# Six pairs' mean and variance computed by ScalarE instead of VectorE, and the one-hot rows of two chunks placed elsewhere

## The reference

```python
h = _layernorm(x, axis=-1) * (1 + ca) + sa
x = x + ga * _L0_attn_ref(h, w_qkv, w_out, b_out)
h = _layernorm(x, axis=-1) * (1 + cb) + sb
gate_probs = softmax(h @ Wg + bg)            # 8 experts, the best two are kept
x = x + gb * sum over the two experts of weight * (gelu(h @ W1 + b1) @ W2 + b2)
```

## Time and profile before

| | |
|---|---|
| median of 3 runs | 812.49 us (812.14 to 812.84) |
| the profiled execution's own time | 813.09 us |
| its span in the profile | 811.3 us |
| PE busy | 755.2 us, 93% of the span |
| DVE busy | 607.8 us, 75% |
| ACT busy | 463.8 us, 57% |
| POOL busy | 339.2 us, 42% |

### The profile page before, as it was taken

How to read it: one execution, slowest core, us unless ns; L and a number is a source line. 1 busy time by engine, 2 the same in 40 slices (tenths; PEclk the granted TensorE clock), 3 DMA queues, 4 the chain that set the end, 5 groups by cost and what they waited for, 6 DMA issues and landing times.

```text
span 811.3 us, 16803 instructions
## 1 busy us (share of the span) xinstructions
PE 755.2 (93%) x5848; PEld 689.0 (85%) x5848; DVE 607.8 (75%) x1325; ACT 463.8 (57%) x841; POOL 339.2 (42%) x291
## 2 busy tenths in 40 slices
PE   4889999999999899984699999999999999999992
PEld 4767778788888679972699999999999999999992
DVE  6899999988899735799576767676676876776652
ACT  4465555756645442359557566665565766765461
POOL 2441414323322101500255565656565555656553
PEclk9999999999999999977699999999999999999997
DMA  7500000000000124590353532626335244333332
GB/s 285 164 1 1 1 1 2 1 2 1 1 2 1 53 102 159 174 234 4 93 147 64 144 64 44 164 43 168 60 91 114 47 120 90 46 48 60 60 48 39
DMA packets 45650, 59.71 MB, mean 74 GB/s; under 512 B 8018, under 2 KB 38804, under 8 KB 45460
## 3 DMA queue, kind: packets, MB, share of 16 engines
q0 software_dynamic: 14400, 21.98, 15.1%
q1 hardware_dynamic: 31188, 36.93, 14.4%
HBM read 40.63 MB, written 18.27 MB: 73 GB/s over the span
## 4 chain that ended last, share of the span: by engine, by line
PE 74%; DVE 16%; issue 5%; ACT 2%; POOL 1%; DMA 1%; SPq 0%; DVEq 0%; POOLq 0%; ACTq 0%
PE ps L1681 24%; PE ps L1695 23%; PE ps L1492 7%; PE ps L1450 6%; PE ps L1513 3%; PE ps L1655 2%; DVE q_max L940 2%; PE ps L1578 2%; PE ps L1501 2%; DVE q_sum L947 2%; DVE k_blk L1050 2%; DVE q_exp L941 1%; ACT at_lo L788 1%; DVE ln_s L904 1%; PE ps L1560 1%
## 5 line engine op out<-in xcount | busy, mean ns | idle before, releaser
L853 ACT ACTIVATE hid<-ps,b_col 128x256 f32<-128x256 f32 (+1 forms) x232 | 105.9, 508 | 114.1 <-PE ps L1681 88.4
L1695 PE MATMUL ps<-w_hi,hid_hi 128*128 128x256 f32 x544 | 153.5, 282 | 0.0
L1695 PE MATMUL ps<-w_lo,hid_hi 128*128 128x256 f32 x544 | 151.2, 278 | 0.0
L1695 PE MATMUL ps<-w_hi,hid_lo 128*128 128x256 f32 x544 | 151.2, 278 | 0.0
L1371 DVE TENSOR_TENSOR hid_lo<-hid,hid_hi 128x512 fp32r<-128x512 f32 (+1 forms) x116 | 90.9, 784 | 76.1 <-ACT hid_hi L857 73.2
L1681 PE MATMUL ps<-xT_hi,w_hi 128*128 128x256 f32 (+1 forms) x464 | 140.9, 304 | 1.6 <-DVE xT_lo L1325 1.6
L1681 PE MATMUL ps<-xT_hi,w_lo 128*128 128x256 f32 (+1 forms) x464 | 140.7, 303 | 0.0
L1681 PE MATMUL ps<-xT_lo,w_hi 128*128 128x256 f32 (+1 forms) x464 | 140.6, 303 | 0.0
L539 POOL TENSOR_TENSOR q_n<-q_exp,q_rec 128x1024 f32<-128x1024 f32 x32 | 60.9, 1904 | 174.7 <-DVE q_rec L948 174.7
L614 POOL DMA_INDIRECT out<-y,y_id x68 | 117.0, 1721 | 40.1 <-POOL y_id L609 16.6
L602 POOL DMA_INDIRECT listed<-xrows,gid x87 | 95.5, 1097 | 42.3 <-POOL gid L598 24.6
(11 more groups left out here) (215 smaller groups left out, 1458.7 us busy)
## 6 DMA issues: line engine op xcount, KB each, us to landing
w_raw<-in_L_ffn_W SPq DMA_DIRECT2D x16, 1024.0 KB
x_all<-in_L_attn_x SPq DMA_DIRECT2D x8, 512.0 KB, 9.3
out<-x_all SPq DMA_DIRECT2D x8, 512.0 KB, 3.0
xrows<-x_all SPq DMA_DIRECT2D x8, 512.0 KB, 4.7
listed<-xrows,gid POOLq DMA_INDIRECT x87
out<-y,y_id POOLq DMA_INDIRECT x68
wqk_raw<-in_L_attn_w_qkv SPq DMA_DIRECT2D x2, 512.0 KB, 6.3
wqk_raw<-in_L_attn_w_qkv SPq DMA_DIRECT2D x1, 1024.0 KB, 10.5
```

Of the source, the lines that this page charges most:

```text
L853: ins = act.activation(hid[:, m, 0:T], src, ACT.Gelu_apprx_tanh, bias=b1_col[:, e, m:m + 1])
L1695: last = pe.matmul(ps[:, bank, 0:D], a, w_, start=m == 0 and st, stop=m == M - 1 and sp_)
```

## The change

DVE no longer takes statistics of pairs 8 to 13. ACT does it in a new function `moments(q)`, after `copy_T(q)`: for each of the two tiles an `Identity` with a constant scale, whose accumulator output is minus a sixteenth of the mean, and, after a wait for both, for each tile a `Square` whose bias is that number and whose accumulator output is the variance. DVE's `root(1)` waits for ACT's twelve variances and has one more instruction. ACT's `lo_hot(0)` moves from behind `copy_T(14)` to behind `copy_T(15)`, `soft(1)` now stands between `lo_hot(0)` and `lo_hot(1)`, and ACT's half of `lo_hot(7)` goes to DVE.

```diff
+ACT_PAIRS = range(8, 14)
...
+            def moments(q):
+
+                n = q - ACT_PAIRS[0]
+                after(act, s_mean, 2 * n)
+                after(act, s_var, 2 * n)
+                for i in range(2):
+                    t = 2 * q + i
+                    act.activation(bn_j[:, i, :], x_all[:, t, :], ACT.Identity, scale=-1.0 / (16 * D), accum_out=bn_m[:, t:t + 1]).then_inc(s_mean, 1)
+                act.wait_ge(s_mean, 2 * n + 2)
+                for i in range(2):
+                    t = 2 * q + i
+                    act.activation(bn_j[:, i, :], x_all[:, t, :], ACT.Square, scale=1.0 / 16, bias=bn_m[:, t:t + 1],
+                                   accum_out=bn_a[:, t, 1:2]).then_inc(s_var, 1)
...
-            def lo_hot(c, ks=range(2)):
+            def lo_hot(c):
...
+                if q in ACT_PAIRS:
+                    moments(q)
                 if q == 9:
                     soft(0)
-                if q == 14:
-                    lo_hot(0)
-            lo_hot(1)
+            lo_hot(0)
             soft(1)
-            lo_hot(2)
-            lo_hot(3)
-            for c in range(GCH, CHUNKS - 1):
+            for c in range(1, CHUNKS - 1):
                 lo_hot(c)
-            lo_hot(CHUNKS - 1, range(1))
...
-                dve.wait_ge(s_stat, q + 1)
+                dve.wait_ge(s_stat, q + 1 if q < ACT_PAIRS[0] else q + 1 - len(ACT_PAIRS))
...
-                if q % (GT // 2):
+                if q % (GT // 2) and q - 1 not in ACT_PAIRS:
                     dve.wait_ge(s_x1, 2 * q)
                     stats(q - 1)
-                    if q % (GT // 2) > 1:
-                        gathered(q - 2)
+                if q % (GT // 2) > 1 and q - 2 not in ACT_PAIRS:
+                    gathered(q - 2)
...
+                if g == 1:
+                    dve.wait_ge(s_var, 2 * len(ACT_PAIRS))
                 link(dve.tensor_scalar(bn_v[:, r], bn_a[:, r, 1], EPS, None, ALU.add))
                 inverse_root(meta[:, r, E], bn_v[:, r], bn_i[:, r], bn_t[:, r])
+                if g == 1:
+                    r = slice(2 * ACT_PAIRS[0], 2 * (ACT_PAIRS[-1] + 1))
+                    dve.scalar_tensor_tensor(meta[:, r, E + 1], bn_m[:, r], 16.0, meta[:, r, E], ALU.mult, ALU.mult)
+                    r = slice(r.stop, TILES)
...
-            lo_hot(CHUNKS - 1, 1)
-            hi_hot(CHUNKS - 1, (1, 0))
+            for k in (1, 0):
+                lo_hot(CHUNKS - 1, k)
+                hi_hot(CHUNKS - 1, (k,))
...
-                    if final and k == 1:
-                        pe.wait_ge(s_loD, 1)
+                    if final:
+                        pe.wait_ge(s_loD, n + 1)
```

More of the change, by code:

```diff
@@ L190, in adaln_block @@
         bn_a = sb("bn_a", [P, TILES, 2], F32, bb_stack)
+        bn_m = sb("bn_m", [P, TILES], F32, bb_stack)
+        bn_j = sb("bn_j", [P, 2, D], F32, bb_stack)
         bn_v = sb("bn_v", [P, TILES], F32, bb_stack)
@@ L248, in adaln_block @@
         s_stat = sem("s_stat")
+        s_mean = sem("s_mean")
+        s_var = sem("s_var")
         s_cT = sem("s_cT")
@@ L785, in lo_hot @@
                 after(act, s_idx, c - GCH + 1)
-                for k in ks:
+                for k in range(2):
                     for i in range(CH):
                         act.activation(at_lo[:, cc, k, i, :], iota_lo[:, :], ACT.Abs, scale=-1.0, bias=spot_lo[:, g, k, cc * CH + i:cc * CH + i + 1]).then_inc(s_abs, 1)
-                act.wait_ge(s_abs, (c * 2 + len(ks)) * CH)
-                one = at_lo[:, cc, 0:len(ks), :, :].rearrange("p k i c -> p (k i c)")
+                act.wait_ge(s_abs, (c * 2 + 2) * CH)
+                one = at_lo[:, cc, :, :, :].rearrange("p k i c -> p (k i c)")
                 act.activation(one, one, ACT.Relu, scale=-1.0, bias=1.0).then_inc(s_loA, 1)
```

## The result

The changed kernel takes 814.92 us (median of 7 runs, 813.29 to 817.41) against 812.55 us of the kernel before (7 runs beside them); ratio 1.0037, 95% interval 1.0026 to 1.0048. It is slower by 0.3 to 0.5%; 815.3 us was forecast. Its profiled execution was the longest of the seven, 817.41 us with a span of 815.7, so 4.3 us above that of before; a second one of the same kernel (816.49 us) is used beside it.

The account below looks back on a forecast made before the run. The prediction took `logits(15)` to gate `scale(1)` and ACT's queue behind the last copy, then sixteen matmuls, to set `ids`. Moving `ids` from 384.32 to 387.1 us (+2.8) gave 815.3 us, range 812.9 to 816.9.

Parts of the forecast that it names:

- What bounds: Before the `ids` write: `scale(1)` waits for `logits(15)`, so DVE's 4.0 us less work becomes idle time.
- The cost of the moments: ACT's added statistics in pairs 8 to 13: 2.29 us a pair, making `copy_T(14)` 0.54 us late.
- the ends 1.53 and 2.67: ACT's microseconds per pair for the statistics: accumulator output free, or a 0.284 us instruction each without overlap.
- The rows: ACT behind the last copy: chunks 0 to 6 without long waits, from 359.26 us to the last Relu's end at 384.06.
- The rival with the high clock: Clock stays high in the ping-pong and under the last matmuls: `ids` +0.5 us, 813.0 us, no difference; chance 0.15.
- DVE's saving: Rival, DVE's work ahead of `ids`: its 4.0 us come through in full, -4 us, 808.5 us; practically excluded.
- PE behind it: PE after ACT's last Relu: sixteen matmuls instead of four, 3.0 us taken (2.1 to 3.9), `ids` at 387.1 us.
- The other arm: PE's ranks and DVE: `place(1)` 0.1 to 0.7 us late, DVE ready at 385.0 to 385.6 us, hidden before `ids`.
- The rest follows rigidly: Everything behind `ids` was to move with its +2.8 us.
- The sum: Whole kernel: `ids` from 384.32 to 387.1 us, +2.8 us, giving 815.3 us against the median.
- No table was loaded for `Square`: Rival on ACT in the pairs: table loads for `Square`, about +16 us, 828; chance 0.10 together with a dear accumulator.
- sooner clock: Rival at the experts' first matmuls: the clock rises sooner, at most 2.8 us won, 812.5 us; chance 0.10.

Follow-up runs that it names:

- both experiments with the transposes ahead: PE transposes pairs 14 and 15 one pair ahead: ratio to the kernel before 1.0004 when added to the changed kernel, 0.9990 when added to the kernel before.
- rows-only kernel: Kernel before with only ACT's low one-hot rows and soft(1) moved and chunk 7's low rows all on DVE, statistics staying on DVE: ratio 1.0036.
- moments only: Kernel before with only the mean and variance of the six pairs moved to ACT, all one-hot rows in their old places: ratio 1.0013.
- before with transposes ahead: Kernel before with only PE's order changed, transposing pairs 14 and 15 one pair ahead: ratio 0.9990, interval 0.9976 to 1.0004.
- the combination: Changed kernel plus transposes of pairs 14 and 15 one pair ahead, ranks(1) before index(1), four of chunk 6's low rows on DVE: 809.33 us, ratio 0.9972.
- the combination without moments: The combination with DVE taking all statistics instead of ACT taking those of six pairs: 813.19 us, ratio 1.0015 to the kernel before.
- index(7) first: Changed kernel with PE multiplying the first half of chunk 7 before chunk 6, so twelve matmuls follow ACT's last Relu: ratio 1.0025 to the kernel before.

## Why the prediction was right

**What bounds.** Right. It said that work removed from DVE has almost nothing to move, as `logits(15)` gates `scale(1)`, and that ACT's queue behind the last copy sets `ids`. The idle 2.45 us, the chain, and both experiments with the transposes ahead show it. DVE was ready for `scale(1)` only 2.8 us sooner, not by the whole saving, as it also waited for PE in the pairs; this changes nothing in the sum, since all of it ended in waits.

**The cost of the moments.** The mechanism was right, the size too large. I took 2.29 us between the ends 1.53 and 2.67; it is 1.92. The small instruction exists, but is 0.19 us long, not the 0.284 of my nearest row, and adds about 0.095 to the pace. So `copy_T(14)` was 0.18 us late instead of 0.54, `copy_T(15)` started at 358.87 instead of 359.26, and the last `Relu` ended at 383.62 instead of 384.06.

**The rows.** Right, and the body of the cost: ACT worked from the last copy to that `Relu` without a gap, and putting chunk 0 back takes away 2.3 us of the 3.0. (One reading of the rows was 0.1 us off: ACT's idle time up to 370.98 is 0.81 us, not 0.9; nothing hangs on it.) What the prediction did not see is that `soft(1)` is a second gate. It noted that DVE arrived at 363.1 just as ACT was free there, but not that a sooner copy would then win nothing. The rival with the high clock (+0.5 us) rested on both DVE's saving and the copy, and the rows-only kernel shows the copy alone to be useless.

**PE behind it.** The sixteen matmuls were undersized: from the end of the `Relu` to `ids` 3.68 us instead of 3.05. I had let the clock rise within them, and it stayed at 0.50 throughout, at which sixteen take 3.59 us; at 1.00 sixteen took 2.09 us of PE's time, in moments only. This 0.63 and the 0.44 on ACT nearly cancel: `ids` at 387.30, 387.1 forecast. That two errors of opposite sign met is luck; the mechanism did not depend on it.

**The other arm.** Right: `place(1)` 0.6 us late (0.1 to 0.7), DVE ready at 385.46 (385.0 to 385.6), hidden by 1.8 us.

**The rest follows rigidly.** Nearly. From `ids` to the first expert's matmul it is 9.82 and 9.47 us in the two executions of the changed kernel, 9.26 before; in the other kernels 9.27 to 9.28 four times (rows only, before with transposes ahead, the combination, the combination without moments) and 9.66 to 9.84 five times. In the longer ones DVE takes up the third tile of gathered rows 6.7 to 7.1 us behind `ids` instead of 6.5. The DMA of the third gather takes 3.34 us in the first execution of the changed kernel and 3.20 in moments only; before, DVE takes that tile up 2.82 us after the gather's start. The whole difference is no more than 0.6 us; why it takes two levels stays open. It may be a part of what moments only costs in time while its `ids` is on time (9.69 there, 0.43 us more than before, of the 1.1 us), but that is argued, not shown. The sum also took every microsecond of `ids` to be one of time. The two profiled executions of the changed kernel are 4.3 and 3.4 us longer than that of before, the ratios make it 3.0 and 3.4 us, and the difference of the first medians is 2.4. The forecast's +2.8 lies among these, but that it met the median within 0.4 us is closer than the sum was good for.

**The rivals.** No table was loaded for `Square`, and no pair was delayed: the copies of pairs 9 to 12 waited for PE. Nor did the experts' stage win by a sooner clock: from its first matmul to the end it is 418.4 and 417.8 us against 417.7. DVE's saving comes through only with the gate open, as said, and then as 2.8 us.

## What to carry to other kernels

When the chain names one engine at a step that needs two, look at how long the other had been ready: if only for a tenth of a microsecond, work taken from the first becomes idle time, and only both edits together move the step. An engine with idle time inside a loop but a full queue behind it has slack only inside: moving 3.4 us of its work from the loop to the queue cost 2.3 us here, though it freed the loop by 0.4. Count also what stands behind the last producer in the consumer's list; here sixteen matmuls instead of four, at the lower clock, were 2.5 us.

## What the hardware showed that was not expected

- An accumulator output on ACT is a second instruction, 187 to 191 ns long for 128 partitions, that adds only about 95 ns to the pace. By shape, in the changed kernel (busy us, mean ns, idle before):

```profile
L792 ACT ACTIVATE bn_j<-x_all,bn_m 128x256 f32<-128x256 f32 x12 | 6.0, 500 | 0.2
L788 ACT ACTIVATE bn_j<-x_all 128x256 f32<-128x256 f32 x12 | 4.8, 406 | 0.0
L788 ACT ACTIVATION_READ_ACCUMULATOR bn_j<-x_all 128x1 f32 x12 | 2.3, 191 | 0.0
L792 ACT ACTIVATION_READ_ACCUMULATOR bn_j<-x_all,bn_m 128x1 f32 x12 | 2.2, 187 | 0.0
```

- The granted clock fell from 1.00 to 0.50 at different steps of the same ping-pong: under `logits(13)` in one execution (index(7) first), ahead of `logits(14)` in before and changed, and ahead of `logits(15)` in rows only. Up to there index(7) first does the same as changed, so the step is not set by the edit alone. Eight logits matmuls take 1.06 us at 1.00 and 1.87 at 0.50, so each step is worth about 0.8 us to what waits for it. PE's row of rows only, where `logits(14)` was still fast:

```profile
354.42 1.06 PE L1594 MATMUL ps<-wg_mod,x1T 128*128 128x8 f32 x8 [0.69 <-ACT x1T L774]
355.33 0.63 PE L1584 MATMUL ps<-ident,x_all 128*128 128x128 f32 x4
356.65 1.87 PE L1594 MATMUL ps<-wg_mod,x1T 128*128 128x8 f32 x8 [0.69 <-ACT x1T L774]
```

- The profiled executions reach the middle stage at either of two moments, 325.5 to 325.6 or 327.0 to 327.3 us, with both kinds among kernels that are alike up to there. Comparing profiles by absolute time would have mistaken 1.5 us of this for an effect.
